# An RNN feeding an LSTM on one core: later x loads, an RNN bias that arrives by a broadcast transfer, and a reordered start on TensorE

## The reference, cut to what matters

```python
def reference(x, cond_1024, L0_cond_Wx, L0_cond_Wh, L0_cond_b, L1_cond_Wx, L1_cond_Wh, L1_cond_b):
    # L0: 512 -> 512          next_h = tanh(prev_h @ Wh + (x @ Wx + b))
    # L1: 512 -> 4 * 512      a = (x @ Wx + b) + prev_h @ Wh
    #     i, f, o = sigmoid(a[0:3]);  g = tanh(a[3])
    #     next_c = f * prev_c + i * g;  next_h = o * tanh(next_c)
    x = x + _L0_cond_ref(x, cond_1024, L0_cond_Wx, L0_cond_Wh, L0_cond_b)
    x = x + _L1_cond_ref(x, cond_1024, L1_cond_Wx, L1_cond_Wh, L1_cond_b)
    return x
```

## Time and profile before

| | before |
|---|---|
| median of 3 runs | 846.36 us (844.5 to 847.37) |
| the profiled execution | 844.77 us, with a span of 843.0 us from the first to the last instruction |
| PE busy | 827.6 us (98% of the span) |
| DVE, ACT, POOL busy | 602.5, 578.9, 289.0 us |
| granted TensorE clock, mean | 0.999 of full speed |
| DMA | 30.70 MB, mean 36 GB/s; 309 and 281 GB/s in the first two of 40 slices |

### The profile page before, as it was taken

The page is one execution under the profiler, slowest core; times in us unless marked ns, Lnnn a source line. Parts: engine busy times, 40 slices in busy tenths (PEclk is TensorE's granted clock), DMA queues, the critical chain, the costliest instruction groups (busy, mean ns, idle before and its releaser), DMA issues.

```text
span 843.0 us, 52000 instructions
## 1 busy us (share of the span) xinstructions
PE 827.6 (98%) x22859; PEld 620.9 (74%) x22859; DVE 602.5 (71%) x1722; ACT 578.9 (69%) x1542; POOL 289.0 (34%) x642
## 2 busy tenths in 40 slices
PE   8899999999999999999999999999999999999997
PEld 5555555677787777877778777787777877778896
DVE  3668778877777776777677777668776776767664
ACT  5986476767676667767767776677767767677652
POOL 1312366723323323333332332333333233333320
PEclk9999999999999999999999999999999999999999
DMA  8801100111001111001111000111110000000001
GB/s 309 281 18 27 29 15 16 28 28 26 19 18 30 29 30 29 16 16 30 29 29 29 23 24 17 29 29 30 29 26 20 17 16 17 16 16 16 11 11 28
DMA packets 40195, 30.70 MB, mean 36 GB/s; under 512 B 5772, under 2 KB 38688, under 8 KB 38688
## 3 DMA queue, kind: packets, MB, share of 16 engines
q1 hardware_dynamic: 39712, 27.27, 11.3%
q10 hardware_dynamic: 256, 0.11, 0.0%
HBM read 18.95 MB, written 8.39 MB: 32 GB/s over the span
## 4 chain that ended last, share of the span: by engine, by line
PE 90%; DMA 4%; DVE 3%; ACT 2%; issue 1%; SPq 0%; ACTq 0%; DVEq 0%
PE ps_l L1290 34%; PE ps_l L1356 29%; PE ps_r L1442 9%; PE ps_r L1462 8%; PE ps_l L1334 3%; PE ps_l L1303 2%; PE ps_l L1323 2%; DMA wxl_raw<-in_L_cond_Wx 2%; DMA whl_raw<-in_L_cond_Wh 2%; DMA whr_raw<-in_L_cond_Wh 1%; PE ps_r L1413 1%; PE ps_r L1424 1%; DVE ig L1092 0%; PE ps_l L1277 0%; DVE fc L1090 0%
## 5 line engine op out<-in xcount | busy, mean ns | idle before, releaser
L496 POOL TENSOR_TENSOR xb<-xb,h_l 128x128 f32<-128x128 f32 x127 | 58.2, 458 | 383.8 <-DVE h_lo L1125 379.4
L1090 DVE TENSOR_TENSOR fc<-gates,c 128x128 f32<-128x128 f32 x128 | 39.6, 309 | 150.4 <-ACT gates L780 136.5
L1356 PE MATMUL ps_l<-whl_raw,wxl_raw 128*32 128x256 f16 x3816 | 131.6, 273 | 0.0
L1290 PE MATMUL ps_l<-whl_hi,hT_hi 128*32 128x512 f16 x1888 | 122.5, 379 | 1.1 <-DVE hT_hi L1109 1.1
L1290 PE MATMUL ps_l<-whl_hi,hT_lo 128*32 128x512 f16 x1888 | 122.5, 379 | 0.0
L1290 PE MATMUL ps_l<-whl_lo,hT_hi 128*32 128x512 f16 x1888 | 122.4, 379 | 0.0
L1356 PE MATMUL ps_l<-wxl_hi,wxl_raw 128*32 128x256 f16 x2544 | 115.8, 273 | 0.0
L1356 PEld LDWEIGHTS ps_l<-whl_raw,wxl_raw 128*32 128x32 f16 x3816 | 102.1, 97 | 2.2 <-issue 0.2
L780 ACT ACTIVATE gates<-ps_l,g_products 128x256 f32<-128x256 f32 x114 | 53.5, 469 | 54.2 <-PE ps_l L1290 54.1
L1290 PEld LDWEIGHTS ps_l<-whl_lo,hT_hi 128*32 128x32 f16 x1888 | 51.1, 97 | 50.8
L1290 PEld LDWEIGHTS ps_l<-whl_hi,hT_lo 128*32 128x32 f16 x1888 | 51.1, 97 | 50.8
(11 more groups left out here) (215 smaller groups left out, 1820.6 us busy)
## 6 DMA issues: line engine op xcount, KB each, us to landing
xb<-in_x SPq DMA_DIRECT2D x128, 64.0 KB, 2.2
out<-xb SPq DMA_DIRECT2D x124, 64.0 KB, 1.8
whl_raw<-in_L_cond_Wh SPq DMA_DIRECT2D x4, 1024.0 KB, 6.6
wxl_raw<-in_L_cond_Wx SPq DMA_DIRECT2D x4, 1024.0 KB, 6.0
wxr_raw<-in_L_cond_Wx SPq DMA_DIRECT2D x1, 1024.0 KB, 5.4
whr_raw<-in_L_cond_Wh SPq DMA_DIRECT2D x1, 1024.0 KB, 7.4
out<-xb SPq DMA_DIRECT2D x4, 48.0 KB, 2.2
wxl_raw<-peaks SPq DMA_DIRECT2D x5, 2.0 KB, 2.6
```

The costliest lines, as they stand in the source:

```text
L496: nc.gpsimd.tensor_tensor(xb[g % NX][:, t, :], xb[g % NX][:, t, :], h_l[s % 2][:, :], ALU.add).then_inc(out_done, 1)
L1290: last = nc.tensor.matmul(ps_l[s % 4][quarter(j), :], (hT_hi, hT_lo)[h_part][:, k, :], gate_slice(whl[w_part][k], j), start=False, stop=(h ...
L1356: last = nc.tensor.matmul(at[quarter(j), :], stationary, weights[:, j, :, :], start=False, stop=(y_part == 1 and k == 1), skip_group_check ...
```

## The change

1. **x groups 3 to 7** are issued once `wxl_raw` 3 (the last chunk) has landed, not once `wxl_raw` 2 has.
2. **The RNN bias** comes by one transfer that repeats each of the 4 rows for 32 partitions, straight into `bias_r` (64 KB written). The product that spread it, and ACT's copy of that, are gone. ACT then seeds `ps_r0` and `ps_r1` for RNN steps 0 and 1 with two copies; it waits for the bias and for a filler in each bank (`r_banks_written`), and PE's first two input products wait for these seeds (`r_first_seeded`). The count of `bias_done` falls by one.
3. **The LSTM bias product** (into `ps_l1`) moves behind the RNN's first input product `product_r(0)`, into iteration 0.
4. **Fillers ahead of `product_r(0)`**: 14 in one row (1, 1, 4, 4, 1, 3 by bank) instead of 6, the bias products, and 6.

```diff
@@ SyncE
             load_x(sp, 2)
-            sp.wait_ge(s_wxl[2], DMA)
+            sp.wait_ge(s_wxl[3], DMA)
             load_x(sp, 3)
             for g in range(4, NX):
                 load_x(sp, g)
@@ ScalarE
             act.dma_start(h0n[:, :], h0.rearrange("b (j u) -> j b u", j=J)).then_inc(s_h0, DMA)
-            act.dma_start(bias_rows_r, bR.rearrange("(j u) -> j u", j=J)).then_inc(s_bias_r, DMA)
+            act.dma_start(bias_r, bR.rearrange("(j u) -> j u", j=J).unsqueeze(1).broadcast_to([J, B, P])).then_inc(s_bias_r, DMA)
...
-            act.wait_ge(bias_mm, 1)
-            nc.scalar.activation(bias_r, ps_l[2][:, 0:P], ACT.Copy).then_inc(bias_done, 1)
+            act.wait_ge(s_bias_r, DMA)
+            act.wait_ge(r_banks_written, 1)
+            for r in (0, 1):
+                nc.scalar.activation(ps_r[r][:, 0:P], bias_r, ACT.Copy).then_inc(r_first_seeded, 1)
...
             def seed_f32(r):
                 act.wait_ge(rnn_h, r - 1)
-                if r == 2:
-                    act.wait_ge(bias_done, 1)
@@ TensorE, product_r
                 if t == 0:
                     pe.wait_ge(x_turned, g + 1)
+                if r < 2:
+                    pe.wait_ge(r_first_seeded, r + 1)
                 wait(pe, r_seeded, r - 1)
@@ TensorE, start
             pe.wait_ge(ident_done, 1)
-            fill(ps_l[3], 3)
-            fill(ps_l[0], 2)
+            fill(ps_r[0], 1)
+            fill(ps_r[1], 1).then_inc(r_banks_written, 1)
+            fill(ps_l[3], 4)
+            fill(ps_l[0], 4)
             fill(ps_end, 1)
-            pe.wait_ge(spread_j_done, 1)
-            pe.wait_ge(s_bias_r, DMA)
-            nc.tensor.matmul(ps_l[2][:, 0:P], spread_j, bias_rows_r, start=True, stop=True).then_inc(bias_mm, 1)
-
-            for r in (0, 1):
-                nc.tensor.matmul(ps_r[r][:, 0:P], spread_j, bias_rows_r, start=True, stop=True)
-            pe.wait_ge(s_bias_l, DMA)
-            nc.tensor.matmul(ps_l[1][:, :], spread_j, bias_rows_l, start=True, stop=True).then_inc(bias_mm, 1)
-            pe.wait_ge(bias_done, 1)
-            fill(ps_l[2], 6).then_inc(banks_written, 1)
+            fill(ps_l[2], 3).then_inc(banks_written, 1)
             product_r(0)
...
                 if k == 0:
+                    pe.wait_ge(spread_j_done, 1)
+                    pe.wait_ge(s_bias_l, DMA)
+                    nc.tensor.matmul(ps_l[1][:, :], spread_j, bias_rows_l, start=True, stop=True).then_inc(bias_mm, 1)
                     fill(ps_pk, 2)
```

More of the change, by code:

```diff
@@ L131, in rnn_lstm_kernel @@
         R_PEAK = 8 + NG
-        bias_rows_l, bias_rows_r, spread_j = pre_l[0:J, :], pre_r[0:J, :], gates[0:J, 0:P]
+        bias_rows_l, spread_j = pre_l[0:J, :], gates[0:J, 0:P]
         yT.append(whl_raw[0][:, 0:TG * P].rearrange("p (k t b) -> p k t b", k=J, t=TG))
@@ L168, in rnn_lstm_kernel @@
         s_bias_r = sem("bias_r_loaded")
+        r_banks_written = sem("rnn_banks_written_first")
+        r_first_seeded = sem("rnn_first_steps_seeded")
         s_bias_l = sem("bias_l_loaded")
@@ L602, in _ @@
             nc.scalar.activation(table_first[:, :], ones[:, 0:1], ACT.Sigmoid)
-            act.wait_ge(bias_mm, 1)
-            nc.scalar.activation(bias_r, ps_l[2][:, 0:P], ACT.Copy).then_inc(bias_done, 1)
+            act.wait_ge(s_bias_r, DMA)
+            act.wait_ge(r_banks_written, 1)
+            for r in (0, 1):
+                nc.scalar.activation(ps_r[r][:, 0:P], bias_r, ACT.Copy).then_inc(r_first_seeded, 1)
             def bias_of_l():
-                act.wait_ge(bias_mm, 2)
+                act.wait_ge(bias_mm, 1)
                 nc.scalar.activation(bias_l[:, :], ps_l[1][:, :], ACT.Copy).then_inc(bias_done, 1)
             def seed_step_0():
-                act.wait_ge(bias_done, 2)
+                act.wait_ge(bias_done, 1)
                 act.wait_ge(banks_written, 1)
@@ L1262, in step_1_input @@
             def step_1_input(k):
-                pe.wait_ge(bias_done, 2)
+                pe.wait_ge(bias_done, 1)
                 pe.wait_ge(yT_done, 2)
```

## The result

| | before, on the same chip | after |
|---|---|---|
| median of 6 runs each | 845.95 us (844.5 to 847.37) | 848.82 us (847.62 to 849.4) |
| ratio, with its 95% interval | | 1.0033 (1.002 to 1.0046) |
| the profiled execution | 844.77 us, span 843.0 | 848.72 us, span 846.9 |

A forecast was written before the change was run, and what follows sets the result against it. The prediction took weight chunk transfers to bound the kernel up to 37.30 us, then TensorE. Terms of -0.4 (x groups) and +0.1 (bias transfer) gave 846.36 - 0.3 = 846.1 us, range 844.0 to 847.9.

The forecast's parts named there:

- PE's start: Before the first RNN input product: bias and seeds ready by 6 us at the latest, ahead of 8.16; cost 0.
- The bias term of the sum: Weight chunk chain at the start: the larger bias transfer delays it by +0.1 us, between 0 and 0.86.
- the sign that I had named: Landing of `whr_raw` and the chunks behind it: within 0.3 us of before; 0.9 late would mean a dearer bias transfer.
- The count of engines, 4: Bias transfer on ACT's queue: a pattern with 4 rows is spread over 4 DMA engines, not 16.
- x groups: Last weight chunk before 37.30 us: its transfer shortens without x groups 3 to 7 beside it, -0.4 us (0.25 to 1.42).
- the rival in which the x packets never held it up: Last weight chunk: an instruction fetch alone delayed it; +0.1 to +0.86 us, 846.5 to 847.2; chance 0.22.
- Later loads of x groups: Groups 3 to 7, issued by about 48 us: delay costs nothing, covered by over 10 us before first use.
- Fillers, seeds, LSTM bias product: PE and ACT before the last chunk: 0 to +0.16 us on the first RNN step, covered by slack; cost 0.
- The clock rival: First RNN step: PE idle until 8.16 falls to 1.2 GHz, step 2.2 us late, about 850 us; chance 0.06.
- "Anything behind 60 us": Kernel behind 60 us: runs as before; otherwise the prediction would be wrong.

The follow-up runs named there:

- experiment 5: Changed kernel with the bias broadcast issued on SP's queue ahead of the RNN weights instead of on ACT's queue: 846.33 us, ratio 1.0012.
- experiment 8: Changed kernel with the bias broadcast issued ahead of the `h0n` load on ACT's queue: 846.37 us, ratio 1.0013.
- experiment 7: Kernel before plus an idle copy of the 64 KB broadcast on ACT's queue, into a tile not needed before 38 us: 850.62 us, ratio 1.0061.
- experiment 9: Kernel of experiment 8 (broadcast ahead of `h0n`) with 26 fillers in place of 14: 846.04 us, ratio 1.0013.
- experiment 1: Kernel before with one edit, x groups 3 to 7 waiting for the last weight chunk: 844.91 us, ratio 0.9996.
- experiment 2: Changed kernel with the old 4-row bias and a spreading product again, the other three edits kept: 844.73 us, ratio 1.0001.
- experiment 3: Changed kernel with 35 fillers ahead of the first input product in place of 14: 847.5 us, ratio 1.0027.
- experiment 4: Changed kernel with the bias broadcast split into four transfers of 32 rows on the same queue: 847.1 us, ratio 1.0021.
- experiment 10: Kernel of experiment 2 (old bias) with the first input product also waiting for `whr_raw`: 848.25 us, ratio 1.0032.
- experiment 6: Kernel of experiment 2 (old bias) with 6 fillers in place of 14: 846.11 us, ratio 1.0003.
- experiment 11: Kernel of experiment 10 (first input product also waiting for `whr_raw`) with 30 fillers in place of 14: 846.16 us, ratio 1.0007.
- experiment 12: Changed kernel with 28 fillers ahead of the first input product in place of 14: 848.04 us, ratio 1.0028.

## Why the prediction was wrong, point by point

The forecast was 846.1 us, "within 0.3%" with 0.86; the time was 848.82, above the range's 847.9.

- **The step that failed** is the one of PE's start: the seeds "wait for the bias, whose old form had been loaded, multiplied and copied from 5.09 on; 0.86 more for the larger transfer makes 6 at the latest, ahead of 8.16. Cost 0". The seed came at 11.80, 5.8 us behind that bound. The 0.86 was the transfer's own engine time on its four engines, as if nothing stood beside it; but from 6 to 10 us two other transfers hold the engines at 93 to 96%, and an engine that takes turns between queues gave a small packet its turn only about once in 0.33 us. The old form moved 4 packets of 512 B; the new one moves 128, 32 on each of its engines, and the ones at the end of the line needed a turn each. (ACT's whole queue went from 256 to 380.) Experiments 5 and 8 show it: the same bytes with no 8 KB packets ahead land at 5.4 and by 4.5.
- **The bias term of the sum** (+0.1, ends 0 and 0.86) was too small too. It was to bound the hold on them. The copy that nobody read held `wxr_raw` up by 1.05 and `whr_raw` by 1.4 us (experiment 7); in after they landed at 10.40 and 12.90, 2.3 us late each, which was the sign that I had named ("if they are 0.9 late, the bias transfer is dearer than I say"). I had called it likely that the chain's links catch up. In after they did, by the last chunk (0.8, 1.6, 0.8 and 0.1 us late from `whl_raw` 1 on), helped by the x groups that were out of its way; in experiment 9 they did not (1.6 late). In the loss of after itself this term has no part that the trace shows, since PE waited for no chunk. The count of engines, 4, was right: that transfer ends on four engines in the trace.
- **x groups**: -0.4 was expected, out of 0.25 to 1.42. The size of the effect on the chunk was about right: it took 6.49 us in experiment 1 in place of 7.40, and from 5.9 to 7.6, 6.8 in the median, in the 12 executions with this edit. As single executions with the x groups early took 7.40 and 7.57, the gain is 0.6 to 0.9 us, with a spread as large. That speaks against the rival in which the x packets never held it up, without ruling it out. But the time did not follow: ratio 0.9996 (0.9987 to 1.0006). What stood behind the wait was nearly as late as the wait: PE and ACT needed 23.5 us from the first tanh, so with a tanh at 11.78 the most to be had was some 2 us, and with the start as it fell in experiments 1 and 2 (13.25 and 12.54) it was 0.4 to 0.5. I had taken that slack from one execution. Later loads of x groups cost nothing, as said; none was waited for.
- **Fillers, seeds, LSTM bias product**: 0 expected, and 1.0001 (0.9989 to 1.0013) measured with all three in place and the old bias. Right. The fillers ended at 7.15, within 5 to 8.
- **The clock rival** (0.06) had the mechanism that came true, for the wrong reason and at the wrong size. It saw PE idle until 8.16 at the latest, and it was idle until 12.22. Its price of 2.2 us for the first step left out the first recurrent product, 0.87 more by its own rows: from the start of `product_r(0)` to the first tanh it is 6.83 us in after and 3.75 in experiment 3, so 3.1. Its time, "about 850", was 1.2 above what came.
- **Against it** I had held that 2.13 us of idle time before 37.30 left the clock up. That row stands, but idle stretches of 2.65, 2.77 and 3.00 us went with a fall in experiments 8, 4 and 10, and experiment 5 shows one with 1.05. The Trainium skill, page "TensorE: Matmul & The Clock Gate", section "What's actually happening", which I had set beside this rival, says that an idle TensorE falls back to 1.2 GHz; the trace agrees, 0.50 granted in the window from 10 to 12 us.
- **"Anything behind 60 us"** ran as before: 3.98 us late at 83.13 and 3.9 at the end.

**What is shown and what is open.** Shown: without the broadcast the loss is gone (experiment 2), and a late start with the half clock brings it back without the broadcast (10), while the clock alone (6) does not and the late start alone (11) does so at most in small part. Open: how the loss is shared where the clock is held up by fillers and the changed kernel still does not recover (3 and 12). For the profiled execution of experiment 3 an estimate from its rows is: a first tanh at 15.88 plus 22.5 us of own work gives 38.4, 1.1 us behind the 37.30 of before, from lateness alone; the pieces with no releaser add 2.0, which makes the 40.42 that came. Without these pieces the last chunk (38.74) would still have held it to 38.9. So lateness, the hold on the chunks and the issue pieces are all in it. How they share the medians of 3 and 12 was not separated, and in experiment 12 the profiled execution was not a typical one. Experiment 9, where the chunk was the bound, lost 0.13%, with an interval that begins at 0. No version beat the kernel before by more than its interval; the nearest is x groups 3 to 7 late alone.

## What to carry to other kernels

A transfer's cost isn't its bytes: count its packets on one engine, and as an upper estimate multiply by the length of a packet of whatever other queue is busy there at that time (32 by 0.33 us here, 10.6, where 9.84 was measured, and 3.2 in an execution where they got in early); a small load that something waits for goes ahead of the bulk on the bulk's own queue, or stays at one packet per engine. Replacing a tiny product by a transfer moves a step from an engine that was idle to the one resource that was full, so ask what bounds the stretch before counting instructions. Where slack is read from one profile, price each delay against the next limit behind the wait too, and add the clock to every idle stretch of PE that a late transfer makes.

## What the runs showed of the hardware

- Two queues on one DMA engine took turns packet by packet: in after seven packets of 512 B from 9.27 to 11.25 us, 0.33 us apart, with an 8 KB packet of 0.31 us behind each; then 0.03 us apart when the other queue was dry. 64 KB took 9.84 us in that execution and 3.2 in another (experiment 12).
- A transfer that waits for its last engine holds the next ones up: `wxr_raw` was complete on 15 engines by 8.54 us and on the last at 10.40 in after, and the share of busy DMA time fell from 94% (8 to 10 us) to 52% (10 to 12 us).
- The granted clock fell to 0.50 in after and experiments 4, 8 and 10 while PE idled (5.07, 2.77, 2.65 and 3.00 us in all), and in experiment 5 with no idle piece longer than 1.05 us ahead of it. When it first rises also varies: at 10.81 us in experiment 1 and at 4.65 before, with the same program on PE. Ahead of the first rise the clock view has no record and shows 1.00: in experiment 6 the products took 1.94 us, the half rate, until 17.4 under such a 1.00. There the length of a known product is the surer sign.
- Packets of 16 KB with PE's instructions ran for 0.9 to 1.5 us each, five or so in the first 42 us of every kernel. In some executions PE stood idle for 0.4 to 1.4 us, waiting for nothing that the profile shows, at most 1.3 us behind the end of one (1.39 us at 19.48 in experiment 11); before and after have the same packets and no such piece. That PE waits for its instructions there is my reading and was not tested. The pieces fall in different places in each kernel and cover differences of half a microsecond and more.
